# Node pass of a graph and feed-forward layer: VectorE's first sum goes to SBUF, and the row gather is issued ahead of the second normalisation

## The reference, cut to what matters

```python
def layer(x, src, dst, W, attn_l, attn_r, W_res, moe0_W1, moe0_b1, moe0_W2, moe0_b2, ...):
    h = layernorm(x)                                   # 50000 nodes x 768 = 12 heads x 64
    hv = h.reshape(n, 12, 64)
    ft = einsum('nhd,od->nho', hv, W)
    e = leaky_relu(sum(ft * attn_l)[src] + sum(ft * attn_r)[dst])      # 25000 edges, sorted by dst
    alpha = softmax of e over the edges of each dst
    agg = segment_sum(alpha[:, :, None] * ft[src], dst, n)
    res = einsum('nhd,od->nho', hv, W_res)
    y = x + relu(agg + res)
    out = y + ffn(layernorm(y))     # gelu(t @ W1 + b1) @ W2 + b2, hidden width 96; 6 first rows: experts
```

## Time and profile before

| | us |
|---|---|
| median of 3 runs | 3027.69 (3019.7 to 3028.32) |
| profiled execution, its own time | 3026.71 |
| its span, first to last instruction | 3024.9 |
| TensorE matmul busy | 2794.6 (92%) |
| VectorE busy | 2601.7 (86%) |
| ScalarE busy | 2186.3 (72%) |
| GpSimd busy | 2123.3 (70%) |
| stores of `out`, issue to landing | 5.6 |

### The profile page before, as it was taken

How to read it: one execution, slowest core, us unless ns; L and a number is a source line. 1 busy time by engine, 2 the same in 40 slices (tenths; PEclk the granted TensorE clock), 3 DMA queues, 4 the chain that set the end, 5 groups by cost and what they waited for, 6 DMA issues and landing times. The chain is left out here.

```text
span 3024.9 us, 67973 instructions
## 1 busy us (share of the span) xinstructions
PE 2794.6 (92%) x21300; PEld 2580.3 (85%) x21300; DVE 2601.7 (86%) x5435; ACT 2186.3 (72%) x4168; POOL 2123.3 (70%) x2027
## 2 busy tenths in 40 slices
PE   1989999999999995589999999999999999999998
PEld 1878888888888883488999999999989999999996
DVE  4678899999999976488999999999989999989995
ACT  0655566666666561388888888998988989989992
POOL 6755566666666720378888888888878888888882
PEclk9999999999999998599999999999999999999998
DMA  8999999888887733489888888888888888888873
GB/s 176 168 182 211 197 217 215 220 217 212 220 218 219 213 120 125 167 289 326 313 311 313 304 306 307 301 300 305 301 281 296 305 294 302 302 288 296 298 259 126
DMA packets 246631, 758.02 MB, mean 251 GB/s; under 512 B 78899, under 2 KB 81203, under 8 KB 246291
## 3 DMA queue, kind: packets, MB, share of 16 engines
q1 hardware_dynamic: 176644, 545.08, 51.2%
q0 software_dynamic: 69312, 209.33, 31.2%
q10 hardware_dynamic: 432, 0.62, 0.1%
HBM read 623.04 MB, written 232.17 MB: 283 GB/s over the span
## 5 line engine op out<-in xcount | busy, mean ns | idle before, releaser
L866 PE MATMUL ps<-wr_bd,arena 128*128 128x128 f32 x4704 | 608.1, 280 | 92.9 <-DVE arena L1192 85.3
L866 PEld LDWEIGHTS ps<-wr_bd,arena 128*128 128x128 f32 x4704 | 567.7, 194 | 113.5 <-issue 111.6
L1187 DVE SCALAR_TENSOR_TENSOR ps<-ps,r_n,arena 128x768 f32<-128x768 f32 x392 | 400.1, 1021 | 114.4 <-DMA arena<-agg_scratch,nrow 93.6
L574 POOL DMA_INDIRECT arena<-agg_scratch,nrow x392 | 438.9, 1120 | 77.6 <-issue 72.4
L656 ACT ACTIVATE t_hi<-ps 128x768 fp32r<-128x768 f32 x392 | 315.0, 804 | 176.3 <-PE ps L711 176.2
L554 POOL TENSOR_SCALAR arena<-csr_neg,mv,r_n 128x768 f32<-128x768 f32 x392 | 386.8, 987 | 50.6 <-PE ps L711 37.7
L613 ACT ACTIVATE arena<-ps 128x512 f32<-128x512 f32 x588 | 312.1, 594 | 138.5 <-PE ps L728 100.4
L1192 DVE SCALAR_TENSOR_TENSOR arena<-ps,arena 128x768 f32<-128x768 f32 x392 | 375.3, 957 | 13.4
L566 POOL TENSOR_SCALAR arena<-arena,nm_n,r_n 128x768 f32<-128x768 f32 x392 | 383.4, 978 | 0.6 <-POOL r_n L582 0.4
L644 ACT ACTIVATE arena<-arena,mv 128x768 f32<-128x768 f32 x392 | 367.7, 938 | 12.7
L1199 DVE TENSOR_TENSOR t_lo<-ps,t_hi 128x768 fp32r<-128x768 f32 x392 | 373.7, 953 | 2.9 <-ACT t_hi L656 2.6
(11 more groups left out here) (201 smaller groups left out, 6556.7 us busy)
## 6 DMA issues: line engine op xcount, KB each, us to landing
arena<-in_x SPq DMA_DIRECT2D x196, 768.0 KB
arena<-in_x_cols SPq DMA_DIRECT2D x392, 384.0 KB
out<-arena SPq DMA_DIRECT2D x195, 768.0 KB, 5.6
agg_scratch<-arena SPq DMA_DIRECT2D x196, 384.0 KB
arena<-in_x,e_slot POOLq DMA_INDIRECT x392
arena<-agg_scratch,nrow POOLq DMA_INDIRECT x392
row_scratch<-e_slot POOLq DMA_INDIRECT x196
nrow<-row_scratch SPq DMA_DIRECT2D x196, 1.0 KB
```

The costliest lines, as they stand in the source:

```text
L574: pool.indirect_dma_start(g_ring[:, g, :], None, agg_d, bass.IndirectOffsetOnAxis(nrow[:, v:v + 1], 0), bounds_check=EP - 1, oob_is_err=Fa ...
L866: last = nc.tensor.matmul(pair(1)[:, i * P:(i + 1) * P], xt_ring[:, g, i * P:(i + 1) * P], wr_bd[:], start=True, stop=True)
L1187: V.scalar_tensor_tensor(pair(1), pair(1), r_n[:, w, k:k + 1], g_ring[:, g, :], ALU.mult, ALU.add).then_inc(s_z1, 1)
```

## The change

L1187 (now L1189) writes its result to the output row `y_ring` in SBUF, not to `pair(1)` in PSUM, and L1192 reads it there. The wait for the earlier store out of that slot (`d_out`) moves in front of the first of the two. TensorE's L866 waits for the first operation (`s_z1`) and no longer for the second (`s_y`). On GpSimd the gather of the agg rows is issued directly behind its base operation, ahead of n2.

```diff
@@ GpSimd, node pass @@
                                            ALU.mult, ALU.mult).then_inc(s_base, 1)
+                    if exists(tb_, NT):
+                        v = (u - L_BASE) % XR
+                        g = (u - L_BASE) % GR
+                        pool.wait_ge(d_x[v // PAIR], 32 * (U // XR * b + (u - L_BASE) // XR + 1))
+                        pool.wait_ge(s_base, tb_ + 1)
+                        settle(pool)
+                        pool.indirect_dma_start(g_ring[:, g, :], None, agg_d,
+                                                bass.IndirectOffsetOnAxis(nrow[:, v:v + 1], 0),
+                                                bounds_check=EP - 1, oob_is_err=False).then_inc(d_g[g], 16)
                     ty = t - L_N2
                     if exists(ty, NT):
...
                         pool.tensor_scalar(n2[:, v % 2, :], y_ring[:, v, :], nm_n[:, w, k:k + 1],
                                            r_n[:, w, PAIR + k:PAIR + k + 1], ALU.add, ALU.mult).then_inc(s_n2, 1)
-                    if exists(tb_, NT):
-                        v = (u - L_BASE) % XR
-                        g = (u - L_BASE) % GR
-                        pool.wait_ge(d_x[v // PAIR], 32 * (U // XR * b + (u - L_BASE) // XR + 1))
-                        pool.wait_ge(s_base, tb_ + 1)
-                        settle(pool)
-                        pool.indirect_dma_start(g_ring[:, g, :], None, agg_d,
-                                                bass.IndirectOffsetOnAxis(nrow[:, v:v + 1], 0),
-                                                bounds_check=EP - 1, oob_is_err=False).then_inc(d_g[g], 16)
@@ TensorE, node pass @@
                         pe.wait_ge(d_xt[g], 16 * (U // GR * b + (u - L_RES) // GR + 1))
-                        at_least(pe, s_y, tr)
+                        at_least(pe, s_z1, tr)
@@ VectorE, node pass @@
                         dve.wait_ge(d_g[g], 16 * (U // GR * b + (u - L_Y) // GR + 1))
-                        V.scalar_tensor_tensor(pair(1), pair(1), r_n[:, w, k:k + 1], g_ring[:, g, :],
+                        if v % PAIR == 0:
+                            at_least(dve, d_out[v // PAIR], 16 * (U // XR * b + (u - L_Y) // XR))
+                        V.scalar_tensor_tensor(y_ring[:, v, :], pair(1), r_n[:, w, k:k + 1], g_ring[:, g, :],
                                                ALU.mult, ALU.add).then_inc(s_z1, 1)
                         dve.wait_ge(s_z1, ty + 1)
-                        if v % PAIR == 0:
-                            at_least(dve, d_out[v // PAIR], 16 * (U // XR * b + (u - L_Y) // XR))
-                        V.scalar_tensor_tensor(y_ring[:, v, :], pair(1), 0.0, x_ring[:, v, :], ALU.max, ALU.add,
+                        V.scalar_tensor_tensor(y_ring[:, v, :], y_ring[:, v, :], 0.0, x_ring[:, v, :], ALU.max, ALU.add,
                                                accum_out=s_st[:, w4, k:k + 1]).then_inc(s_y, 1)
```

## The result

| | before | changed |
|---|---|---|
| median, same chip | 3023.69 us (4 runs) | 3175.55 us (4 runs) |
| ratio | | 1.0507 (1.0480 to 1.0534) |
| profiled execution, its span | 3024.9 | 3172.4 |
| a pair of tiles, mean over the node pass | 8.70 | 9.50 |

The changed kernel is 5.1% slower, 152 us. The forecast was 3023 us with a range of 2960 to 3100; the result lies outside it. All of the loss is in the node pass: base (L554) starts there 382 times in 1810.7 us, so a pair takes 1810.7/381 x 2 = 9.50 us, and (9.50 - 8.70) x 196 = 157 us. That count leaves out the fill and the end of the pass; VectorE's L1176, whose 392 records are all there, runs from 1302.5 to 3142.0 us against 1306.0 to 2993.2 before, which is 152 us more.

What follows compares the result with a forecast made beforehand. Level VectorE and TensorE plus late second gathers were taken as the bound. The new pair, 8.59 with 0.10 of stalls, gave 8.69 against 8.71 us, over 196 pairs -4 us: 3023 us, range 2960 to 3100.

Steps and rivals of the forecast that it cites:

- What bounds the kernel before: Node pass: VectorE (8.13 us a pair) and TensorE (8.20) level; the rest to 8.71 nearly all late gathers.
- a fixed 7.35: Second gather of a pair: time from issue to use taken as 7.35 us, against 6.33 available.
- Part 1: Gather ahead of n2 on GpSimd: 0.98 us more room for the second gather, wait for base priced at 0.17.
- the pair walked: Node-pass pair followed through every engine; new second gather at 6.45 us, VectorE's end at 8.59, next n2 7.6 to 8.6.
- Part 2: First sum (L1187, now L1189) to SBUF on VectorE: price 0; TensorE's release 0.9 us sooner, worth nothing.
- The hidden cost of L1192: VectorE's L1192 reads two SBUF rows, so it and GpSimd shut each other out: 0.46 us a pair.
- The sum: Node-pass pair: 8.59 plus 0.10 of remaining stalls, 8.69 against 8.71 us; -4 us in all, 3023 us.
- Rival (b): GpSimd becomes the bound, its gather issue held behind L1192: 9.2 us a pair, +92 us, 3119 us; chance 0.23.
- Rival (a): VectorE's L1192 isn't held by GpSimd's reads: 8.38 us a pair, -65 us, 2962 us; chance 0.22.
- the balanced case: Likeliest case, node pass: gather stalls exchanged for a wait at L1192; 2986 to 3060 us, chance 0.55.
- What would show it: Node-pass signs: gather stalls under 20 us, L1192 1.5 us behind L1189 in first tiles, undisturbed pairs 8.5 to 8.7 us.
- wrong altogether: Signs of failure in the node pass: gather stalls near 0.5 us a pair, or VectorE or GpSimd operations themselves longer.

Runs made afterwards that it cites:

- e11: Kernel before with VectorE's three statistics (L1210 to L1212) moved up between L1187 and L1192; 2939.4 us, ratio 0.9708.
- e6: Kernel before with VectorE's three statistics (L1210 to L1212) moved ahead of L1199; 2994.5 us, ratio 0.9911.
- e2: Kernel before with only the gather moved ahead of n2, the sum still in PSUM; 3159.0 us, ratio 1.0496.
- e13: e2 without the nop between the gather's waits and the gather; 3180.0 us, one run.
- e14: Kernel before in its old order, the gather also waiting for the n2 directly ahead of it, whose data it doesn't use; 3190.7 us, ratio 1.0605.
- e12: e2 with the previous tile's gather issued in the same place, its base a step old; 3361.2 us, one run.
- e7: e2 with VectorE's three statistics moved ahead of L1199; 3137.6 us, ratio 1.0351.
- e1p: e1 with L1192's second input the product in PSUM instead of the x row, and TensorE waiting for L1192; 3026.4 us, ratio 1.0004.
- e4: Changed kernel with TensorE's residual matmul waiting for L1192 again instead of L1189; 3169.0 us, ratio 1.0520.
- e1: Changed kernel with the gather back behind n2, so only the sum to SBUF and the earlier release remain; 3172.5 us, ratio 1.0553.
- e3: Changed kernel with L1192's x row replaced by the product in PSUM, and TensorE waiting for L1192; 3158.9 us, ratio 1.0490.

## Why the prediction was wrong

- **What bounds the kernel before**: right. Late rows of the second gather gave the place to push, and e11 shows the price: with the stalls gone the pair is 8.27, near TensorE's 8.20. The time from issue to use is not a fixed 7.35, though: over the first sums that had to wait, it is 7.4 us in the median in the kernel before (8 of 10 between 6.7 and 8.2) and 8.2 in e6.
- **Part 1**: this is the step that failed. "The wait of the issue for its own base is no longer covered by n2; the 0.17 stood there even with n2 between the earlier trace rows, so I take 0.17 again." The row was one where the awaited operation had ended a whole n2 earlier; it could not price a wait on the operation directly ahead. It is 0.83 to 0.87 (changed kernel, e2, e13), 0.93 in the old order (e14), and 0.17 where the wait is old (e12). Twice 0.67 us a pair went on an engine whose list had, in the pair walked, 8.13 - 7.78 = 0.35 to spare. By the prediction's own reckoning that is a pair of 7.78 + 2 x 0.67 = 9.12, (9.12 - 8.71) x 196 = +80, some 3108 us: over half of the loss, and outside the range.
- **A term that was missing**: VectorE's statistics, held while n2 runs. The walk itself laid n2 (7.6 to 8.6) over the end of VectorE's pair (8.59) and priced nothing there. In the pair above they cost 0.33 and 0.65 us, and the power, which waits for the last of them, starts 0.18 after n2 for it; e7 takes two thirds of the hold away and gains 0.18 a pair.
- **Part 2**: the change of output costs nothing, as said (e1p); the earlier release is worth nothing, as said (e4).
- **The hidden cost of L1192**: right in kind and in size, 0.46 forecast, 0.41 measured (0.42 a pair in the mean), and e1 shows the other direction. In the changed kernel it is hidden, because VectorE is held at its statistics anyway; e3 removes it and gains nothing that can be told from the intervals. In the old order the same two inputs cost 5.5% (e1), by holding GpSimd as well (n2 0.31, base 0.13, gather 0.11 us each in the mean). The 0.41 is their price in the new order only.
- **The sum**: 8.69 was walked for a pair of 9.37. The walk had the second gather start at 6.45; in fact it starts at 7.30 (1846.97 - 1839.67). Each engine's list should have been summed for itself as well: 7.78 + 2 x 0.67 = 9.12. The 0.25 from there to 9.37 is read afterwards, 0.18 in front of the power and 0.07 in small gaps; most of the 0.13 from there to the mean of 9.50 is that the gap before a gather is 0.89 in the mean and not 0.84.
- **Rival (b)**, GpSimd becomes the bound, had the right engine, 9.2 us and 3119 us against 9.50 and 3175, but its cause was another, a gather issue held behind L1192. Its own signs came out against it: the second gather's record is 1.10 us, not 1.8 (from 1310 to 2900 us, 6 of 334 gathers took over 1.3), and the power still waits for the statistics, 0.18 each time. That it came nearest is luck: two blocks of 0.7 were taken for a cause that is hardly there, and two of 0.67 came from another.
- **Rival (a)**, VectorE isn't held by GpSimd's reads: refuted by the 1.37 us record. The sign that was written down to tell it from the balanced case was a bad one, see below.
- **What would show it**: gather stalls under 20 us came true; the first gather's record of 1.6 did not (1.14), since it starts only when L1192 is done; undisturbed pairs of 8.5 to 8.7 did not. L1192 was to start 1.5 us behind L1189 in the first tile; it starts 1.04 behind (1840.54 to 1841.58), which is the sign given for (a). The hold is there all the same: it makes the record longer and does not move its start. What was to mean "wrong altogether", operations that get longer themselves, did appear, in L1192 by 0.41 and in L1212 by 0.65.

## What to carry to other kernels

In these runs, a gather's issue that waits for another instruction of its own engine is cheap when other work stands between (0.17 us) and dear when none does (0.83 to 0.93): before moving a transfer's issue up behind its producer, price the exposed wait, by a row where an issue truly waits for its neighbour, and add it to that engine's own list. When three engines are within 5% of each other, sum each list per period, not only the chain. A late start can be cured at the other end: three small statistics moved up gave 2.9% (e11) where moving the gather lost 5.0% (e2).

## What the runs showed of the hardware

- A gather's issue on GpSimd that has to wait for the operation directly ahead starts 0.83 to 0.93 us after that one's record ends (e2, e13, e14), against 0.17 where the wait is old; a compute operation (base behind the power) needs 0.21. Removing the nop does not remove it (0.87 in e13). Which part of the preparation this is stays open.
- VectorE with two SBUF inputs and GpSimd's 768-element reads exclude each other both ways: L1192 lost 0.41 us behind base, n2 lost 0.78 behind L1192 (e1). A held instruction starts on time and has a longer record. In the changed kernel the release comes before the record's end: from 1310 to 2900 us, 163 L1192 start with 0.57 us of base left and lose 0.41, and 130 start with 0.17 left and lose 0.01. In e1, where n2 follows base at once, a start with 0.16 left lost 0.19; why is open. This is the rule of the Trainium skill, "SBUF — State Buffer", section "Who interferes with whom", by which whoever is first keeps the other out for its whole instruction. The runs agree on who waits, but the wait is shorter, 0.41 where the whole record would give 0.57.
- A gather's issue is held by such an operation too: in e1, 36 of the 37 gathers that start within 0.75 us behind the start of an L1192 take over 1.2 us, where 1.09 to 1.15 is usual in the kernel before.
- VectorE's statistics over two elements, with one SBUF input each, were held in part. L1212 takes 0.81 us in place of 0.16, until n2 ends, and L1210 0.49, until 0.28 us after the gather's issue ends; L1211, the same operation on another buffer, takes 0.16 with n2 running beside it, and why is open. Where GpSimd was idle they took 0.16 (e11). The same section says that such an operation can take the shared pair in its faster mode; L1212 agrees with that, L1211 doesn't show it, and no run here tries a form without it.
